# Message layers of a graph network: the next group's block numbers are read between a group's seven products

## The chip, the cores and the metric

One core of one Trainium2 chip. The metric is the device time of one execution in microseconds (us); lower is better. Three runs of the kernel before gave 5613.98, 5620.78 and 5626.88 us; their median, 5620.78 us, is the time before.

## What is computed

Four residual graph layers over 50,000 nodes with 64 features and 25,000 edges sorted by destination. The change touches the sums over edges of the first two layers (the message layers):

```python
# layer 0                                    # layer 1
messages = relu(concat(x[src], x[dst]) @ W_msg + b_msg)   ;   messages = x[src] * norm[:, None]
agg = segment_sum(messages, dst, num_segments=num_nodes)
```

The matrix products in front of layer 0's relu are made per node beforehand, so per edge only two gathered rows are added.

## The kernel before, in words

The edges lie in 200 blocks of 128, the nodes in tiles of 128. Because edges are sorted by destination, the sum over edges walks a path through (block, tile) pairs: from one item of the path to the next either the block or the tile goes up by one. There are 602 items for each layer, in 86 groups (LOTS) of seven (LOT). An item is one product: a one-hot matrix (edge lane against node lane, 128 by 128, fp32) times the block's messages (128 by 65 in layer 0, 128 by 64 in layer 1, fp32), added into one of seven slots of a PSUM bank.

`plan_items` packs each group's part of the path into one integer before the layers: the low eight bits are the group's first block number, and six more bits say for items 1 to 6 whether the block number goes up by one.

`edge_sums` is called once for each of the two layers. Its engines run side by side, tied by semaphores:

- POOL gathers the rows of four blocks at a time (a chunk; 50 chunks) with indirect DMAs, L736 and L738 in layer 0 (two per block), L741 in layer 1 (one per block). It then adds and clamps them (L748, L750) or multiplies them by a factor (L753) and raises `msg_ready` by one per chunk.
- DVE makes the seven one-hot matrices of a group in one instruction (L794, two buffers), once the products of the group before last are done, and adds the partial sum of a tile that two groups share (L800) once a group's products are done (`multiplied`).
- ACT reads the group's first tile number from a table into a register, copies that partial sum (L770), and after DVE's addition copies the group's bank into `sums` (L773), then raises `placed`.
- PE (L810 to L826) takes the group's integer from SBUF into a register (L812), clears the bank with a product of zeros (L817, which waits for `placed`), waits for the one-hots and for the chunk of the group's last block (L818 to L820), and issues seven products (L825). Both the messages' address and the slot's address of each product are computed from registers. An fp32 product runs as two passes, so seven products are 14 matmul records.

`item_blocks` (L670 to L676) builds the seven block numbers as expressions of the group's integer: mask, then for each item shift, mask and add. Register arithmetic is emitted when a value is first used. For the block numbers that is the wait at L819, whose value is the chunk of the last block. Arithmetic of neighbouring instructions is packed into one (FUSED_REGOPS in the trace) where it can be; the rest stands alone (ALU_OP). Before each product the addresses are computed at L825. All of these, with TENSOR_LOAD, SEQ_ASSERT (the check of the loaded value's bounds) and EVENT_SEMAPHORE, are instructions of PE's sequencer, which the trace marks PEldq. PE's sequencer takes its instructions in the order of the program.

The later part of the kernel (`diffuse`) uses registers that are changed in place, as the changed code does: `Counts.read` (L2077) copies such a register with `snap` before a use, and `finished` (L2080, L2081) adds one to it.

After each `edge_sums` all engines meet and `node_update` reads `sums`.

Of the kernel before, what the change touches and what calls it, by code (L numbers as in the profile page):

```python
# [29 lines left out]
CHUNKS = 2 * -(-EDGES // (2 * CH))  # L30
# [6 lines left out]
BLOCKS = EP // P  # L37
HALF = BLOCKS // 2
LOT = 7
LOTS = 2 * -(-(TILES + BLOCKS - 1) // (2 * LOT))  # L40
ITEMS = LOT * (LOTS + 1)
BLOCK_BITS = 8
# [625 lines left out]
                step(None, at(0, LAST))  # L668


def item_blocks(engine, path):

    blocks = [engine.snap((path & ((1 << BLOCK_BITS) - 1)).with_bounds(max_val=BLOCKS - 1))]
    for q in range(1, LOT):
        blocks.append(engine.snap((blocks[-1] + ((path >> BLOCK_BITS + q - 1) & 1)).with_bounds(max_val=BLOCKS - 1)))
    return blocks  # L676


def edge_sums(nc, net, layer, sums):


# [9 lines left out]
    n = f"e{layer}_"  # L691
    with ExitStack() as ctx:
        ctx.callback(nc.all_engine_barrier)
        def sb(name, shape, dt=F32):
            return ctx.enter_context(nc.sbuf_tensor(n + name, shape, dt))
# [6 lines left out]
        plan = sb("plan", [1, LOTS + 1], I32)  # L702
# [12 lines left out]
        loaded, cleared, added, msg_ready, hot_ready, multiplied, before_ready, joined, placed, pe_turn, act_turn = map(sem, names)  # L715
        n_loads = 6 if two else 5
        with nc.Block() as block:
            @block.sync
            def _(sp):
                sp.dma_start(src[:, :], net.src_cols[:, :]).then_inc(loaded, 16)  # L720
                if two:
                    sp.dma_start(dst[:, :], net.dst_cols[:, :]).then_inc(loaded, 16)
                sp.dma_start(lane[:, :], net.item_lane[:, :]).then_inc(loaded, 16)
                sp.dma_start(numbers[:, :], net.dram["c_iota"][:, 0:P]).then_inc(loaded, 16)
                sp.dma_start(plan[:, :], net.lot_plan[:, :]).then_inc(loaded, 16)
                sp.dma_start(first[:, :], net.lot_first[:, :]).then_inc(loaded, 16)
# [79 lines left out]
            @block.tensor  # L806
            def _(pe):
                pe.wait_ge(loaded, 16 * n_loads)
                pe.wait_ge(cleared, 1)
                for g in range(LOTS):  # L810
                    s = g % 2
                    path = pe.value_load(plan[0:1, g:g + 1], min_val=0, max_val=(1 << BLOCK_BITS + LOT - 1) - 1)  # L812
                    blocks = item_blocks(pe, path)
                    slots = [pe.snap((blocks[0] + q - b).with_bounds(min_val=0, max_val=LOT - 1)) for q, b in enumerate(blocks)]
                    chunk = pe.snap((blocks[-1] >> 2) + 1)
                    pe.wait_ge(placed, g + 1)
                    nc.tensor.matmul(ps[s][:, 0:LOT * wide], net.ones3[:, :], nothing[:, 0:LOT * wide], start=True, stop=False)  # L817
                    pe.wait_ge(hot_ready, g + 1)  # L818
                    pe.wait_ge(msg_ready, chunk)  # L819
                    pe.sem_inc(pe_turn, 1)  # L820
                    by_slot = ps[s][:, 0:LOT * wide].rearrange("p (u c) -> p u c", c=wide)
                    for q, (b, u) in enumerate(zip(blocks, slots)):
                        rows = msg[:, bass.ds(b, 1), 0:wide].rearrange("p b c -> p (b c)")
                        to = by_slot[:, bass.ds(u, 1), :].rearrange("p u c -> p (u c)")
                        last = nc.tensor.matmul(to, hot[s][:, q, :], rows, start=False, stop=q == LOT - 1)  # L825
                    last.then_inc(multiplied, 1)  # L826


# [1715 lines left out]
```

## Time and profile before

| what | value |
|---|---|
| median of three runs | 5620.78 us |
| the profiled execution's own time | 5624.62 us |
| its span in the profile | 5622.8 us |
| layer 0, first to last product | 836.9 to 1516.2 us |
| layer 1, first to last product | 1903.7 to 2306.0 us |
| PE / DVE / ACT / POOL busy share of the span | 60% / 48% / 19% / 50% |
| matmuls in the two stages | 2408 of 12060 |
| granted clock of PE in both stages | 0.50 |

The table's stages come from the timeline; the clock is the share of full speed that was granted, and 0.50 is the 1.2 GHz level. A line such as "L825" is a line of the kernel; "idle before <- X" says what ended the idle time of the engine in front of an instruction; "issue" means that nothing the profile shows was waited for. Records marked with a q after the engine's name are the sequencer's, and are not counted as busy.

### The profile page before, as it was taken

How to read it: one execution, taken by the hardware profiler on the slowest of the kernel's cores; microseconds unless marked ns; L12 is line 12 of the kernel's file. 1: busy time of each engine (PE TensorE's matmuls, PEld its weight loads, DVE VectorE, ACT ScalarE, POOL GpSimd, SP SyncE). 2: the span in 40 equal slices, each digit the busy share in tenths (PEclk: the TensorE clock that was granted, in tenths of full speed). 3: DMA queues.
4: the chain of work that ended last, by engine and by line, in shares of the span. 5: the costliest groups of instructions: out<-in, count | busy, mean ns of one | idle time of the engine just before them, and what ended most of it. 6: DMA issues, size and time to landing. Idle time of an engine off the chain costs nothing. (4 is left out here: it accounts for less than half of the span.)

```text
span 5622.8 us, 58211 instructions
## 1 busy us (share of the span) xinstructions
PE 3387.3 (60%) x12060; PEld 2043.7 (36%) x12060; DVE 2719.4 (48%) x6625; ACT 1086.5 (19%) x2025; POOL 2834.5 (50%) x2360
## 2 busy tenths in 40 slices
PE   3664544444499577675667665777744555555534
PEld 1222433433477466552222223555531222222212
DVE  6996551111155422364555453777774444444423
ACT  0232320101122111121222222333321111111100
POOL 0462017777511584234777772122126888787740
PEclk7776555555555555555555555555556777676765
DMA  5222430010155210252111112121112222233210
GB/s 192 82 69 100 179 118 19 19 20 20 39 151 157 52 22 13 99 210 72 23 23 23 23 23 79 70 98 79 72 61 33 30 29 30 28 31 29 28 17 3
DMA packets 350982, 346.67 MB, mean 62 GB/s; under 512 B 264934, under 2 KB 290267, under 8 KB 350835
## 3 DMA queue, kind: packets, MB, share of 16 engines
q1 hardware_dynamic: 229596, 272.37, 14.8%
q0 software_dynamic: 107888, 60.13, 8.7%
q10 hardware_dynamic: 13350, 12.40, 0.6%
q8 instruction: 69, 1.13, 0.1%
q14 instruction: 79, 0.64, 0.0%
HBM read 172.86 MB, written 175.50 MB: 62 GB/s over the span
## 5 line engine op out<-in xcount | busy, mean ns | idle before, releaser
L825 PE MATMUL e_ps<-e_msg,e_hot 128*128 x2408 | 553.9, 421 | 449.4 <-POOL e_msg L750 324.9
L825 PEld LDWEIGHTS e_ps<-e_msg,e_hot 128*128 128x128 f32 x2408 | 526.5, 330 | 522.9 <-issue 522.9
L2208 POOL DMA_INDIRECT out<-d_out,d_end x356 | 592.6, 1665 | 172.0 <-issue 167.1
L2252 PE MATMUL d_pl<-d_hot,d_fields 128*65 128x512 f32 x712 | 501.8, 870 | 0.0
L800 DVE TENSOR_TENSOR e_ps<-e_ps,e_before 128x65 f32<-128x65 f32 (+1 forms) x172 | 40.0, 233 | 871.0 <-PE e_ps L825 871.0
L736 POOL DMA_INDIRECT e_msg<-from_src,e_src x200 | 208.0, 1040 | 374.3 <-DMA e_first<-lot_first 320.3
L1971 POOL DMA_INDIRECT list<-s_rec,s_place x200 | 197.7, 988 | 290.6 <-DVE s_place L1887 234.7
L1671 POOL TENSOR_TENSOR u_tg<-u_t,norms 128x1792 f32<-128x1792 f32 x14 | 55.5, 3964 | 441.6 <-DVE u_t L1506 441.6
L1309 PE MATMUL u_po<-bias_parts,ones 3*128 3x256 bf16 x392 | 148.8, 380 | 213.7 <-issue 95.9
L741 POOL DMA_INDIRECT e_msg<-h1d,e_src x200 | 223.5, 1118 | 101.8 <-issue 54.9
L915 POOL DMA_INDIRECT a_ends<-h,a_src x200 | 220.7, 1104 | 102.7 <-issue 60.6
L738 POOL DMA_INDIRECT e_near<-from_dst,e_dst x200 | 227.1, 1136 | 61.0 <-issue 61.0
L773 ACT ACTIVATE sums<-e_ps 128x455 f32 (+1 forms) x172 | 94.0, 547 | 828.1 <-DVE e_ps L800 828.1
L1393 ACT ACTIVATE u_zt<-u_pt 128x256 f32<-128x256 f32 (+1 forms) x392 | 162.8, 431 | 461.7 <-PE u_pt L1303 461.4
L2233 PE MATMUL d_pc<-d_liveb,d_before 128*128 128x4 bf16 x89 | 14.8, 166 | 389.5 <-DVE d_prod L2350 389.1
L2252 PEld LDWEIGHTS d_pl<-d_hot,d_fields 128*65 128x65 f32 x712 | 140.1, 212 | 291.7 <-issue 291.7
L922 POOL DMA_INDIRECT agg<-a_out,a_end x200 | 204.6, 1023 | 80.5 <-issue 61.5
L2200 POOL DMA_INDIRECT d_near<-term,d_rec x196 | 190.3, 971 | 83.6 <-issue 41.8
L2244 PE MATMUL d_pr<-ident,d_scan 65*128 65x65 f32 x356 | 63.8, 334 | 275.8 <-DVE d_scan L2373 275.8
L915 POOL DMA_INDIRECT a_ends<-h,a_dst x200 | 191.5, 957 | 60.9 <-issue 60.9
L2200 POOL DMA_INDIRECT d_near<-terms,d_rec_idx x168 | 163.7, 975 | 97.5 <-DMA d_rec_w<-list_w 48.7
L2347 DVE SCALAR_TENSOR_TENSOR d_live<-d_near,d_inside 128x4 f32<-128x4 f32 x89 | 14.7, 165 | 393.4 <-DMA d_near<-term,d_rec 226.7
(359 smaller groups left out, 8152.6 us busy)
## 6 DMA issues: line engine op xcount, KB each, us to landing
u_z<-h SPq DMA_DIRECT2D x28, 896.0 KB, 6.2
x<-sums SPq DMA_DIRECT2D x28, 896.0 KB, 7.8
u_x<-x SPq DMA_DIRECT2D x28, 896.0 KB, 7.4
terms<-s_zeros SPq DMA_DIRECT2D x16, 812.5 KB, 11.8
s_key_row<-src_key SPq DMA_DIRECT2D x50, 256.0 KB
h1d<-u_h SPq DMA_DIRECT2D x14, 910.0 KB, 9.4
u_z<-h1d SPq DMA_DIRECT2D x14, 910.0 KB, 4.6
term<-u_h SPq DMA_DIRECT2D x14, 910.0 KB, 3.6
```

The lines of the kernel that those rows point to most:

```text
L736: pool.indirect_dma_start(msg[:, b, 0:C], None, net.from_src[:, :], bass.IndirectOffsetOnAxis(ap=src[:, b:b + 1], axis=0)).then_inc(gather ...
L738: pool.indirect_dma_start(near[c % 2][:, j, :], None, net.from_dst[:, :], bass.IndirectOffsetOnAxis(ap=dst[:, b:b + 1], axis=0)).then_inc( ...
L741: pool.indirect_dma_start(msg[:, b, :], None, net.h1d[:, :], bass.IndirectOffsetOnAxis(ap=src[:, b:b + 1], axis=0)).then_inc(gathered[c % ...
L825: last = nc.tensor.matmul(to, hot[s][:, q, :], rows, start=False, stop=q == LOT - 1)
L915: pool.indirect_dma_start(ends[s][:, j, half * C:(half + 1) * C], None, net.h2[:, :], bass.IndirectOffsetOnAxis(ap=rows, axis=0)).then_inc ...
L922: pool.indirect_dma_start(net.agg2[:, :], bass.IndirectOffsetOnAxis(ap=end[s][:, j:j + 1], axis=0), out[s][:, j, :], None, bounds_check=NP ...
L1309: nc.tensor.matmul(po[b][:, 0:J * C], net.ones3[:, :], net.bias_parts[:, which, :, :].rearrange("k j c -> k (j c)"), start=True, stop=False)
L1393: nc.scalar.activation(zt[b][:, :], pt[b][:, 0:TURNS * P], ACT.Copy).then_inc(zt_ready, 1)
L1971: pool.indirect_dma_start(net.lists0[:, :], bass.IndirectOffsetOnAxis(ap=place[:, t:t + 1], axis=0), rec[:, t, :], None).then_inc(scattere ...
L2200: pool.indirect_dma_start(near[s][:, j, :], None, table[:, :], bass.IndirectOffsetOnAxis(ap=row, axis=0)).then_inc(gathered[s], 16)
L2208: pool.indirect_dma_start(net.out[:, :], bass.IndirectOffsetOnAxis(ap=end[s][:, j:j + 1], axis=0), out[s][:, j, 0:C], None, bounds_check=N ...
L2252: last = nc.tensor.matmul(pl[0:WEIGHT + 1, :], fields[:, j, :], hot[:, j, :], start=j == 0, stop=j == J - 1)
```

## The change

Registers for the path, for the chunk and for two sets of seven block numbers are allocated. A new function `read_item(g, q)` takes item q of group g from the path into the set g % 2. It is called seven times before the loop for group 0, and in the loop once behind each product, for the same item of the next group. The slots' addresses are computed in place, and `item_blocks` goes.

```diff
-def item_blocks(engine, path):
-
-    blocks = [engine.snap((path & ((1 << BLOCK_BITS) - 1)).with_bounds(max_val=BLOCKS - 1))]
-    for q in range(1, LOT):
-        blocks.append(engine.snap((blocks[-1] + ((path >> BLOCK_BITS + q - 1) & 1)).with_bounds(max_val=BLOCKS - 1)))
-    return blocks
...
+                path_at = pe.alloc_register(n + "path")
+                chunk_at = pe.alloc_register(n + "chunk")
+                block_at = [[pe.alloc_register(f"{n}block{s}_{q}") for q in range(LOT)] for s in range(2)]
+
+                def read_item(g, q):
+                    row = block_at[g % 2]
+                    if q == 0:
+                        path = pe.value_load(plan[0:1, g:g + 1], min_val=0, max_val=(1 << BLOCK_BITS + LOT - 1) - 1)
+                        pe.reg_mov(path_at, path >> BLOCK_BITS)
+                        pe.reg_mov(row[0], path & ((1 << BLOCK_BITS) - 1))
+                    else:
+                        path = pe.snap(path_at, min_val=0, max_val=(1 << LOT - 1) - 1)
+                        pe.reg_add(row[q], row[q - 1], path & 1 if q == 1 else (path >> q - 1) & 1)
+                    if q == LOT - 1:
+                        pe.reg_mov(chunk_at, (pe.snap(row[q], min_val=0, max_val=BLOCKS - 1) >> 2) + 1)
+                for q in range(LOT):
+                    read_item(0, q)
                 for g in range(LOTS):
                     s = g % 2
-                    path = pe.value_load(plan[0:1, g:g + 1], min_val=0, max_val=(1 << BLOCK_BITS + LOT - 1) - 1)
-                    blocks = item_blocks(pe, path)
-                    slots = [pe.snap((blocks[0] + q - b).with_bounds(min_val=0, max_val=LOT - 1)) for q, b in enumerate(blocks)]
-                    chunk = pe.snap((blocks[-1] >> 2) + 1)
+                    blocks = [pe.snap(r, min_val=0, max_val=BLOCKS - 1) for r in block_at[s]]
                     pe.wait_ge(placed, g + 1)
                     nc.tensor.matmul(ps[s][:, 0:LOT * wide], net.ones3[:, :], nothing[:, 0:LOT * wide], start=True, stop=False)
                     pe.wait_ge(hot_ready, g + 1)
-                    pe.wait_ge(msg_ready, chunk)
+                    pe.wait_ge(msg_ready, pe.snap(chunk_at, min_val=1, max_val=CHUNKS))
                     pe.sem_inc(pe_turn, 1)
                     by_slot = ps[s][:, 0:LOT * wide].rearrange("p (u c) -> p u c", c=wide)
-                    for q, (b, u) in enumerate(zip(blocks, slots)):
+                    for q, b in enumerate(blocks):
+                        u = (blocks[0] + q - b).with_bounds(min_val=0, max_val=LOT - 1)
                         rows = msg[:, bass.ds(b, 1), 0:wide].rearrange("p b c -> p (b c)")
                         to = by_slot[:, bass.ds(u, 1), :].rearrange("p u c -> p (u c)")
                         last = nc.tensor.matmul(to, hot[s][:, q, :], rows, start=False, stop=q == LOT - 1)
+                        if g + 1 < LOTS:
+                            read_item(g + 1, q)
                     last.then_inc(multiplied, 1)
```

## Rows read from the trace of the kernel before

**Rows 1.** The page, costliest groups: busy, mean ns | idle before <- releaser.

```profile
L825 PE MATMUL e_ps<-e_msg,e_hot 128*128 x2408 | 553.9, 421 | 449.4 <-POOL e_msg L750 324.9
```

**Rows 2.** Line 825 by its source line, layer 1 alone (1900 to 2310 us).

```profile
L825 PEldq FUSED_REGOPS  x1118: 42/143/178, 1903.4 to 2304.7; - x187
its engine sat idle before it (us, times) until:
  issue: 196.0, 158
  POOL e_msg L753: 13.7, 14
```

**Rows 3.** Timeline of PE in layer 1: start us, length us, what, idle before.

```profile
1908.44 3.22 PE L825 MATMUL e_ps<-e_msg,e_hot 128*128 x14 [1.05 <-issue]
1911.60 0.55 PE L817 MATMUL e_ps<-e_nothing,ones 3*128 3x448 bf16 x1
1913.05 3.22 PE L825 MATMUL e_ps<-e_msg,e_hot 128*128 x14 [0.91 <-issue]
```

**Rows 4.** Timeline of POOL at the end of its work in layer 1.

```profile
2189.33 1.08 POOL L753 TENSOR_TENSOR e_msg<-e_msg 128x256 f32<-128x256 f32 x1 [2.56 <-DMA e_msg<-h1d,e_src]
```

**Rows 5.** One group of layer 1, PE's sequencer, 2298.15 to 2302.75 us, line by line: count, ns min/median/max, first and last start.

```profile
L825 PEldq FUSED_REGOPS  x12: 42/92/156, 2298.2 to 2300.0; - x12
...
L812 PEldq TENSOR_LOAD <-e_plan x1: 298/298/298, 2300.1 to 2300.1; - x1
...
L819 PEldq ALU_OP  x8: 32/32/36, 2300.8 to 2302.1; - x8
L819 PEldq FUSED_REGOPS  x6: 52/54/67, 2301.1 to 2302.2; - x6
...
L820 PEldq EVENT_SEMAPHORE  x1: 51/51/51, 2302.3 to 2302.3; - x1
...
L825 PEldq FUSED_REGOPS  x1: 166/166/166, 2302.5 to 2302.5; - x1
L825 PEldq ALU_OP  x1: 36/36/36, 2302.7 to 2302.7; - x1
```

**Rows 6.** Timeline around that group: start us, length us, engine, what.

```profile
2301.29 0.55 PE L817 MATMUL e_ps<-e_nothing,ones 3*128 3x448 bf16 x1
2301.47 0.23 DVE L800 TENSOR_TENSOR e_ps<-e_ps,e_before 128x64 f32<-128x64 f32 x1 [3.42 <-PE e_ps L825]
...
2301.82 0.54 ACT L773 ACTIVATE sums<-e_ps 128x448 f32 x1 [3.13 <-DVE e_ps L800]
2302.78 3.22 PE L825 MATMUL e_ps<-e_msg,e_hot 128*128 x14 [0.94 <-issue]
```

**Rows 7.** Register work elsewhere in the kernel, by source line: ns min/median/max.

```profile
L2077 PEldq FUSED_REGOPS  x89: 35/35/46, 4232.9 to 5487.1; - x89
...
L2080 DVEq FUSED_REGOPS  x89: 59/71/214, 4249.9 to 5504.0; - x89
...
L2088 PEldq FUSED_REGOPS  x10: 152/158/172, 4232.0 to 5516.4; - x10
...
L2088 DVEq FUSED_REGOPS  x10: 207/226/234, 4232.1 to 5516.3; - x10
...
L2133 PEldq FUSED_REGOPS  x10: 73/78/88, 4231.0 to 5504.0; - x10
```

**Rows 8.** Timeline of PE in the middle of layer 0.

```profile
1400.62 3.22 PE L825 MATMUL e_ps<-e_msg,e_hot 128*128 x14 [6.14 <-POOL e_msg L750]
...
1414.24 3.22 PE L825 MATMUL e_ps<-e_msg,e_hot 128*128 x14 [9.91 <-POOL e_msg L750]
```

**Rows 9.** Timeline at the end of layer 0.

```profile
1498.83 3.22 PE L825 MATMUL e_ps<-e_msg,e_hot 128*128 x14 [7.45 <-POOL e_msg L750]
...
1499.15 0.84 POOL L750 TENSOR_SCALAR e_msg<-e_msg 128x256 f32<-128x256 f32 x1 [0.19 <-issue]
...
1512.97 3.23 PE L825 MATMUL e_ps<-e_msg,e_hot 128*128 x14 [0.91 <-issue]
```

## The prediction

> **What bounds the kernel now.** The page comes first: the change touches only the two message layers, and there only PE's products of L825 and the register work around them [rows 1]. Of PE's 449 us of idle time in front of them, 325 end on a message of L750, that is, on POOL in layer 0. So layer 0 goes at POOL's pace, and PE's register work is free there except behind the last message. Layer 1 is different: by the view of that line in layer 1 alone, 196 us of idle time end on "issue" in 158 pieces, and only 13.7 us on POOL in 14 pieces [rows 2], each about 1 us, the size of the gap in every group. POOL is done at 2190.4 us [rows 4] and PE goes on to 2306.0 [rows 6]. Layer 1 is PE's own.
>
> What is it in PE? In the timeline one group starts 4.61 us behind the one before: 3.22 us of 14 passes, about 0.5 of the product of zeros, which overlaps them a little, and a gap of 0.91 us on "issue" (1.05 one group earlier, 0.94 in the last group) [rows 3, 6]. The sequencer's records of one group [rows 5] tell what the gap is. Behind the last product's issue L812 runs from 2300.1 to 2300.8, L819's 14 records from 2300.8 to 2302.3, the semaphore instruction to 2302.5, the first addresses to 2302.8, where the first pass starts [rows 6]. The other 12 address packs, two per product, take the 1.9 us from 2298.2 to the next L812. Together 4.6 us, the whole pitch: **the sequencer is never idle, and the array waits for it**. The array needs only some 3.7 us per group. Over the layer the pitch is (2302.78 - 1908.44) / 84 = 4.69 us, counting 84 groups between those two starts [rows 3, 6].
>
> From this follows how the change is to be priced. Work that is moved from one place of a serial queue to another, when the queue is what bounds, gains nothing. Only the sum of the sequencer's work per group counts, and so I count instructions.
>
> **What stays.** The load, its check and its assertion (0.7 us), the semaphore instruction, the addresses of seven products and the issues are all still there. The slot's expression is the one that was already computed at L825, so its 13 packs and one single stay. No DMA, no wait and no other engine's instruction is added or moved.
>
> **What goes.** The 14 records of L819: 1.5 us per group [rows 5]. Their executions add up to 8 x 33 + 6 x 54 = 588 ns, so each has 65 ns around it that no record shows. That is the price rule that I use: duration plus 65 ns. The counts also tell how the work is packed. Six items need 6 shifts, 6 masks and 6 additions; with the first mask and the chunk's shift and addition these are 21 operations. In 8 singles and 6 packs they fit only if each of the 7 masks stands alone, with one shift alone, and additions join shifts: a mask is never packed.
>
> **What comes**, per group:
> - Masks: 7 as before, now parted by products, alone: 7 x 0.10 = 0.70 us.
> - Item 0: a shift and a copy into the path register. The nearest row is an addition followed by a copy, 78 ns (L2133 in [rows 7]): 0.14 us.
> - Item 1: a copy of the path register by snap, alone: 0.10 us.
> - Items 2 to 6: copy and shift, a pack. Nearest: copy and addition 35 ns (L2077 in [rows 7]), addition and shift 54 ns [rows 5]: 45 + 65, 0.11 us, five times 0.55.
> - The copy of block 0 and the additions of items 1 to 5 join the address pack of the following product, which grows by one member. An address is block x width x 4 + base, the slot's number (block 0 + q - block) x width x 4 + base: eight operations in packs of six and two. These take 143 and 42 ns [rows 2], so 25 ns a member: 6 x 0.02 = 0.12 us.
> - At the group's border 12 operations meet: item 6's addition, copy, shift, addition and copy for the chunk, then seven snap copies of the block registers, which a register changed in place needs and the old expressions did not. They need two packs. The longest pack of DVE's L2080 (three additions, three copies and a product, by the program) takes 214 ns; DVE's L2088 takes 226 where PE's takes 158 [rows 7], so about 150 on PE, somewhat more for a fuller pack: 190, and 120 for the rest. With 65 each, 0.44 us.
> - The chunk's snap before the wait, alone, as it follows the wait for the one-hots: 0.10 us.
>
> Sum 2.15 us against 1.5: **+0.65 us of sequencer work per group**. The pitch becomes about 5.35 us.
>
> Bounds. Cheap end: no copy costs anything (all values used straight from their registers), and what is left are 7 masks (0.70), 6 shifts alone (0.60), additions in packs (0.14) and a pack of three for the chunk (0.13): 1.57, +0.1. Dear end: nothing joins the address packs, so 6 members cost a single each (0.60 in place of 0.12): +1.1. I take the middle case, since the rows of L2077 show such copies as instructions, and the packs as joining.
>
> **Layer 1**: 85 groups read the next one, and group 0 is read ahead of the loop, behind the wait for the cleared sums, as its integer is now; nothing covers that. All of it is the sequencer's time: 86 x 0.65 = 56 us.
>
> **Layer 0**: in the middle POOL covers it. Two groups that wait for messages start 13.6 us apart [rows 8]; a chunk of 4 blocks feeds 86 x 4 / 200 = 1.7 groups, 9 us of PE even at the new pitch. Behind the last message (end of L750 at 1500.0) four groups are worked off, with starts from 1498.83 to 1512.97 [rows 9]; three pitches grow: 3 x 0.65 = 2 us.
>
> What waits for the spread-out products? After product 0 the sequencer has about 1.3 us of load and arithmetic, after each other some 0.55 us, so a group's products end about 4.4 us after their start, not 3.2. DVE's addition and ACT's copy are over 0.9 us after that end [rows 6]; DVE's one-hots come between, and all of them serve the group after next: 5 us of room, no new wait.
>
> By these terms the profiled execution goes from its own 5624.6 us (span 5622.8) by 58 to 5683 us. The median of the runs is 3.8 us under that execution: **5679 us**.
>
> The Trainium skill, Advanced Engine Details and Errata, section Sequencer Loop, adds that other engine instructions can be read and queued while the sequencer's microcode executes one. By that rule alone moved register work would hide and the time be that of the first rival below. The rows show products queued so (the product of zeros is released by the array and not by the sequencer), but none whose own addresses are still to be computed.
>
> **Rivals.**
> 1. **The gap closes: faster.** If the sequencer were held back while seven products are in flight (by a queue in front of the array), work put there would fill lost time, and the 0.94 us gap [rows 3, 6] would go: 85 x 0.94 = 80 us, 5541. POOL would allow it: done at 2190 us [rows 4], PE then at about 2226. It decides if the sequencer has more than 0.65 us of held time among the products. For it: the gap is real, and "issue" sounds like latency. Against it: the 12 packs among the products are half of 42 and half of 143 ns, with 65 each 1.9 us in all, and the rows give 1.9 from 2298.2 to 2300.1 [rows 5]: nothing is held. The array takes 3.22 / 7 = 0.46 us per product and the sequencer 0.31, so it already runs ahead. Chance 0.07.
> 2. **It hardly matters, or it doesn't do what it says:** the compiler computes the values where they are used as before, or all copies vanish. 89 groups' worth at 0 to 0.1 us: 5621 to 5630. Against it: registers changed in place can't be read later. Chance 0.09.
> 3. **Dearer:** nothing is packed over the border of an item; 89 x 1.1 = 98, 5719. For it: a pack whose copies come late in it is slow (78 against 35 ns, L2133 against L2077 [rows 7]). Chance 0.14.
> The forecast has 0.70.
>
> **How the numbers follow.** A measurement of this kernel can tell 0.2%, 11 us, from no change. Slower by more: the forecast, rival 3 and a little: 0.84. Within 11 us: 0.08. Faster: rival 1 in full or in part, 0.08. The range reaches from the cheap end (5630) to the dear end (5719) and leaves out rival 1 and most of rival 2.
>
> **What would show it.** Right: layer 1's pitch about 5.3 us, layer 1 some 56 us longer, 14 records fewer before the wait, one or two records more behind each product, and the passes in pairs with gaps, the largest behind product 0 where the load stands; behind the product of zeros a gap of about 0.3 us instead of 0.94 (1.2 us of sequencer work behind the last product's issue, 0.9 of it under the array); layer 0 longer by about 2 us; everything behind unchanged. Wrong: a pitch under 4.69, or a layer 1 whose 14 passes still take 3.22 us while the gap shrinks.

## The result, and the profile after

The changed kernel takes 5641.2 us (median of 7 executions, 5637.8 to 5653.95) against 5620.78 (7 executions, 5613.98 to 5626.88): a ratio of 1.0039, 95% interval 1.0029 to 1.0049. The three times given for the kernel before are the lowest, the median and the highest of its seven. It is slower, as forecast, but by 20.4 us where 58 were forecast. Its profiled execution took 5641.14 us (span 5639.3).

A table by stage shows at once where that stands. The stages run from a layer's first product of zeros to its last product, and are read from the timelines; "one layer" means experiments 1 and 2 below.

| stage, us | before | after | layer 0 alone changed | layer 1 alone changed |
|---|---|---|---|---|
| ahead of layer 0 | 834.5 | 837.5 | 837.7 | 835.1 |
| **layer 0's sums** | 681.7 | **638.8** | 637.9 | 681.7 |
| between | 384.8 | 387.0 | 383.1 | 385.0 |
| **layer 1's sums** | 405.0 | **466.0** | 405.2 | 466.0 |
| all behind | 3316.8 | 3310.1 | 3311.4 | 3317.3 |
| span | 5622.8 | 5639.3 | 5575.3 | 5685.1 |

Layer 1 lost 61.0 us, and the forecast was 56. Layer 0, forecast to lose 2, **gained 42.9**. The page's line for the products [rows 1] shows both in one row:

```profile
L832 PE MATMUL e_ps<-e_msg,e_hot 128*128 x2408 | 720.6, 443 | 291.9 <-POOL e_msg L742 175.1 <-issue 110.7
```

The idle time that ends on POOL's message of layer 0 (L742 is L750 of before) fell from 325 to 175 us. Idle time that ends on "issue" did not fall: it is 110.7 us, as before. What grew is the busy column, from 553.9 to 720.6 us, since the short gaps between one product's passes and the next product's are counted there. A view by line is therefore read together with the timeline, here of PE in layer 1:

```profile
2305.57 3.49 PE L832 MATMUL e_ps<-e_msg,e_hot 128*128 x12 [0.66 <-issue]
2309.06 0.55 PE L823 MATMUL e_ps<-e_nothing,ones 3*128 3x448 bf16 x1
2309.64 0.66 PE L832 MATMUL e_ps<-e_msg,e_hot 128*128 x2
2310.92 3.68 PE L832 MATMUL e_ps<-e_msg,e_hot 128*128 x12 [0.62 <-issue]
2314.57 0.55 PE L823 MATMUL e_ps<-e_nothing,ones 3*128 3x448 bf16 x1
```

Before, 14 passes stood together in 3.22 us behind a gap of about 0.9 [rows 3, 6]. Now product 0 stands alone (0.66 us), 0.62 us of idle time follow, and the other six take 3.68 us, 0.61 each instead of 0.46. The gap behind the product of zeros is gone. The pitch (from one group's first product to the next group's) is (2326.01 - 1863.86) / 85 = 5.44 us, counted over the 85 pitches of the layer; counted in the same way before, from 1903.69 to 2302.78 us, it was 4.70: **+0.74 us per group**, 63.1 us in 85 pitches. The stage grew by 2.1 us less, since it starts with the first product of zeros, and group 0's numbers are now computed ahead of that: from there to the first product it takes 0.6 us instead of 2.7. The sequencer's records from 2309.6 to 2315.2 us, against [rows 5]:

```profile
L809 PEldq TENSOR_LOAD <-e_plan x1: 297/297/297, 2309.7 to 2309.7; - x1
...
L810 PEldq FUSED_REGOPS  x1: 98/98/98, 2310.3 to 2310.3; - x1
L811 PEldq ALU_OP  x1: 36/36/36, 2310.5 to 2310.5; - x1
L811 PEldq FUSED_REGOPS  x1: 200/200/200, 2310.6 to 2310.6; - x1
L813 PEldq FUSED_REGOPS  x5: 63/63/64, 2311.6 to 2313.9; - x5
L813 PEldq MOVE  x1: 29/29/29, 2311.1 to 2311.1; - x1
L814 PEldq ALU_OP  x6: 32/32/32, 2311.2 to 2314.1; - x6
L814 PEldq FUSED_REGOPS  x6: 169/169/213, 2311.3 to 2314.2; - x6
L821 PEldq FUSED_REGOPS  x1: 90/90/90, 2314.4 to 2314.4; - x1
L825 PEldq MOVE  x1: 29/29/29, 2314.6 to 2314.6; - x1
L832 PEldq FUSED_REGOPS  x6: 42/42/42, 2310.8 to 2313.8; - x6
```

These show all that was forecast of the packing: seven masks alone (the `ALU_OP` records of L811 and L814), five copies packed with shifts (L813's `FUSED_REGOPS`) and the first one alone (its `MOVE`), the chunk's copy alone (L825), and additions that joined the next product's addresses (L814's packs). From one load to the next there are 35 records of 3.04 us together instead of 32 of 2.47. Three records more at 65 ns each and 0.57 us more of durations make 0.77, against the 0.74 of the pitch.

Where did layer 0's gain come from? That layer goes at POOL's pace, so POOL is the engine to read. First the kernel before, POOL's costliest lines from 834 to 1502 us (busy, mean ns | idle before):

```profile
L738 POOL DMA_INDIRECT e_near<-from_dst,e_dst x192 | 219.6, 1144 | 58.6 <-issue 58.6
L736 POOL DMA_INDIRECT e_msg<-from_src,e_src x191 | 199.4, 1044 | 51.7 <-issue 51.7
L750 POOL TENSOR_SCALAR e_msg<-e_msg 128x256 f32<-128x256 f32 x49 | 41.4, 844 | 61.4 <-issue 61.4
L748 POOL TENSOR_TENSOR e_msg<-e_msg,e_near 128x256 f32<-128x256 f32 x49 | 33.9, 691 | 1.0
```

The same of the changed kernel:

```profile
L728 POOL DMA_INDIRECT e_msg<-from_src,e_src x192 | 187.3, 975 | 51.9 <-issue 51.9
L730 POOL DMA_INDIRECT e_near<-from_dst,e_dst x192 | 184.7, 962 | 58.6 <-issue 58.6
L742 POOL TENSOR_SCALAR e_msg<-e_msg 128x256 f32<-128x256 f32 x49 | 43.2, 881 | 63.6 <-issue 63.6
L740 POOL TENSOR_TENSOR e_msg<-e_msg,e_near 128x256 f32<-128x256 f32 x49 | 34.7, 708 | 1.0
```

The gathers (indirect DMAs, whose duration on POOL is that of their issue) fell from 419.0 to 372.0 us. The two arithmetic lines and the idle time in front of one of them gave back 1.8 + 0.8 + 2.2 us. The sum is -42.2 us, and layer 0's gain 42.9. And the change has no instruction on POOL. The timeline of the kernel before shows beside what the gathers took longer:

```profile
1400.28 1.03 POOL L736 DMA_INDIRECT e_msg<-from_src,e_src  x1 [0.17 <-issue]
...
1402.87 0.95 POOL L736 DMA_INDIRECT e_msg<-from_src,e_src  x1 [0.30 <-issue]
...
1404.09 1.08 DVE L794 TENSOR_TENSOR e_hot<-e_lane,e_numbers 128x896 f32<-128x896 f32 x1
1404.12 1.86 POOL L738 DMA_INDIRECT e_near<-from_dst,e_dst  x1 [0.30 <-issue]
```

Gathers of 0.95 us start every 1.25 us. One of them starts 0.03 us behind the start of DVE's one-hots and takes 1.86 us. In layer 0 of before, 60 gathers take over 1.3 us; what they take above 0.95 comes to 51 us. In the changed kernel there is none. Its timeline at the same point of a chunk:

```profile
1376.44 0.84 POOL L742 TENSOR_SCALAR e_msg<-e_msg 128x256 f32<-128x256 f32 x1 [1.20 <-issue]
...
1377.88 0.66 PE L832 MATMUL e_ps<-e_msg,e_hot 128*128 x2 [7.48 <-POOL e_msg L742]
...
1379.17 3.53 PE L832 MATMUL e_ps<-e_msg,e_hot 128*128 x12 [0.63 <-issue]
...
1382.56 0.95 POOL L728 DMA_INDIRECT e_msg<-from_src,e_src  x1 [0.30 <-issue]
...
1382.96 1.08 DVE L786 TENSOR_TENSOR e_hot<-e_lane,e_numbers 128x896 f32<-128x896 f32 x1
...
1383.81 1.05 POOL L730 DMA_INDIRECT e_near<-from_dst,e_dst  x1 [0.30 <-issue]
```

The one-hots wait for the group's products, the products wait for the message, and the message comes from POOL. So the one-hots keep a fixed distance to POOL's next gathers. The spread-out products now end 4.82 us behind their start instead of 3.22, and the one-hots start 5.68 us behind the message's end (1377.28) instead of 3.98 (1404.09 - 1400.11): 1.7 us later. At that point a gather has already been running for 0.40 us and is not held, and the next starts 0.85 us behind the one-hots and is held by only 0.1. The distance is nearly the same in every chunk: over the 47 messages that PE waits for it is 3.98 us each time in the kernel before, and 5.55 to 5.75 us, 5.61 at the median, in the changed one.

In layer 0 of the kernel before and of the changed one, a gather that starts x us behind the one-hots' start (x from 0.04 to 0.95) ends 0.81 to 0.83 us behind their end, whatever x is: it is held by about 0.95 - x. One that started ahead of them is not held. In the kernel before the border is sharp and lies where its gathers start: all those between 0 and 33 ns take 0.95 us, all from 35 ns on are held (1.87 us at 35 ns), and of the three at 34 ns one is free and two are held. Of the 60 held gathers 33 (30.1 us) belong to the first one-hots behind a message and 27 (20.8 us) to the second.

The clamping in L742 is held too, which is 1.8 us of what layer 0 gave back. In the changed kernel 18 of its 49 runs in layer 0 start 0.16 to 0.41 us before a second group's one-hots end, end about 0.70 us behind them and take up to 1.11 us instead of 0.84. Before, no run starts beside the one-hots, and all take 0.84 or 0.85. One of the 18:

```profile
1103.37 1.08 DVE L786 TENSOR_TENSOR e_hot<-e_lane,e_numbers 128x896 f32<-128x896 f32 x1
...
1104.06 1.09 POOL L742 TENSOR_SCALAR e_msg<-e_msg 128x256 f32<-128x256 f32 x1 [1.21 <-issue]
```

From here two theories compete. **A**: the hold as just told is layer 0's gain, and layer 1's loss is the sequencer's work; the two parts are independent. **B**: something else of the new order (PE's spread passes, the earlier load, a different start of the stage) speeds POOL up, and the one-hots' place goes along by chance. Four experiments (5, 6, 7 and 8) shared a chip on which the kernel before took longer too (5811.75 us). There PE's sequencer stands still for over 0.4 us at a time in layer 1 (102 times, 70 us together, in experiment 6; never in the profile of before), and code of layer 1 that is the same as before took 427, 510 and 437 us in experiments 5, 6 and 7. So layer 0 alone is read in their traces, together with its held gathers, and 7 and 8 were run again elsewhere. Ratios leave out executions in the chip's slower state, and the profiled execution of experiment 6 (5886.16 us) was one of those.

### The profile page after: what moved, and what is told of

Its sections match the earlier page's. It is cut to its first block and busy times, and to the rows that moved or that the text cites. A ratio compares the mean times of both kernels' runs of the same rounds, so it can differ in the third digit from the quotient of the medians.

```text
span 5639.3 us, 58727 instructions
## 1 busy us (share of the span) xinstructions
PE 3555.8 (63%) x12060; PEld 2115.2 (38%) x12060; DVE 2715.8 (48%) x6625; ACT 1088.9 (19%) x2025; POOL 2772.1 (49%) x2360
## 5 line engine op out<-in xcount | busy, mean ns | idle before, releaser
L832 PE MATMUL e_ps<-e_msg,e_hot 128*128 x2408 | 720.6, 443 | 291.9 <-POOL e_msg L742 175.1
L832 PEld LDWEIGHTS e_ps<-e_msg,e_hot 128*128 128x128 f32 x2408 | 602.2, 311 | 456.4 <-issue 402.0
L728 POOL DMA_INDIRECT e_msg<-from_src,e_src x200 | 194.9, 974 | 374.6 <-DMA e_first<-lot_first 320.6
L733 POOL DMA_INDIRECT e_msg<-h1d,e_src x200 | 203.6, 1018 | 101.9 <-issue 54.9
L730 POOL DMA_INDIRECT e_near<-from_dst,e_dst x200 | 192.2, 961 | 61.0 <-issue 61.0
L1670 POOL TENSOR_TENSOR u_a<-sums,u_z 128x1792 f32<-128x1792 f32 x14 | 45.4, 3243 | 337.3 <-DMA u_x<-x 337.3
```

The costliest lines, as they stand in the source:

```text
L728: pool.indirect_dma_start(msg[:, b, 0:C], None, net.from_src[:, :], bass.IndirectOffsetOnAxis(ap=src[:, b:b + 1], axis=0)).then_inc(gather ...
L730: pool.indirect_dma_start(near[c % 2][:, j, :], None, net.from_dst[:, :], bass.IndirectOffsetOnAxis(ap=dst[:, b:b + 1], axis=0)).then_inc( ...
L733: pool.indirect_dma_start(msg[:, b, :], None, net.h1d[:, :], bass.IndirectOffsetOnAxis(ap=src[:, b:b + 1], axis=0)).then_inc(gathered[c % ...
```

## The experiments

**1 and 2: each half of the change alone.** `edge_sums` takes the changed PE block for one layer and the old one for the other.

```diff
             @block.tensor
+            if two:          # experiment 2: if not two
+                ...          # PE as in the changed kernel
+            else:
                 ...          # PE as before
```

> The changed PE code in layer 0 alone, the old one in layer 1. Theory (POOL's gathers in layer 0 are held up by DVE's one-hots when a gather starts just behind the one-hots' start, and the change moved the one-hots by some 1.7 us against the gathers): layer 0 takes about 639 us instead of 682, no gather over 1.3 us, and the whole about 5578 us, faster than both kernels. Rival (the 43 us of layer 0 were chance of one execution, or belong to something else in the program): layer 0 stays at 682 and the whole at 5621 to 5623.

> The changed PE code in layer 1 alone, the old one in layer 0. Theory (PE's sequencer bounds layer 1 and has 0.74 us more to do per group): layer 1 takes 466 us instead of 405, layer 0 682 as before, the whole about 5682 us. Rival (layer 1's loss depends on when layer 0 ended or on the two together): anything else.

Measured: 5578.88 us with layer 0 changed (ratio 0.993, 0.9914 to 0.9947, to 5622.21 for the kernel before), and 5683.3 with layer 1 changed (1.0108, 1.0092 to 1.0125). The stage table has their stages: each half moves its own layer and nothing else. -43.3 and +61.1 make +17.8, against +20.4 for the whole change. So the two effects are independent, and the second run is what the forecast described: it forecast 5679 for both layers, and 5683 is what layer 1 alone does.

**3: the kernel before, with the one-hots about 0.4 us later in layer 0.** DVE waits for its own work to end (`drain`) and clears 200 columns of an unused PSUM bank in front of the one-hots. Nothing of PE is changed.

```diff
                     if not start:
                         v.wait_ge(multiplied, g)
+                        if two:
+                            v.drain()
+                            for i, w in enumerate((200,)):
+                                nc.vector.memset(idle[:, i, 0:w], 0.0)
                     nc.vector.tensor_tensor(hot[s], ...)
```

> PE's code as before; in layer 0 DVE drains and clears 200 columns of an idle PSUM bank before each one-hots, so that they start about 0.3 us later. Theory of the phase: most gathers that started 0 to 0.1 us behind the one-hots' start now start 0.2 to 0.3 us ahead of it and are not held; layer 0 gets 40 to 50 us shorter, the whole about 5575 us. Rival (the gain of layer 0 comes from PE's spread products, not from the one-hots' place): layer 0 stays within 3 us of 682.

Measured: 5614.69 us (0.9986, 0.9976 to 0.9995). Layer 0 took 662.2 us, 19.5 less: under half of the 40 to 50 that A expected, and well outside the 3 us of no change. Two stretches of its timeline say why only half:

```profile
1402.44 0.95 POOL L739 DMA_INDIRECT e_near<-from_dst,e_dst  x1 [0.30 <-issue]
1402.80 1.07 DVE L799 TENSOR_TENSOR e_hot<-e_lane,e_numbers 128x896 f32<-128x896 f32 x1
1403.70 0.99 POOL L737 DMA_INDIRECT e_msg<-from_src,e_src  x1 [0.30 <-issue]
...
1407.43 1.07 DVE L799 TENSOR_TENSOR e_hot<-e_lane,e_numbers 128x896 f32<-128x896 f32 x1
1407.50 1.82 POOL L739 DMA_INDIRECT e_near<-from_dst,e_dst  x1 [0.30 <-issue]
```

The first group behind a message is freed: the gather at 1402.44 was under way, the next starts 0.90 us behind the one-hots. But a second group often follows at once, and its one-hots, 4.63 us later, now start 0.07 us ahead of a gather. My expectation had looked at the first group alone: its held gathers fell from 33 to 1, but the second's rose from 27 to 32. Layer 0 keeps 34 long gathers (over 1.3 us) with an excess (what they take above 0.95 us) of 30 us instead of 51, and its 19.5 us of gain are those 21. The whole gained 7.5 us and not 19.5: `diffuse` took 1408.1 us in this execution and 1398.1 before, and why isn't known.

**4: the check of the loaded value's bounds is left out on PE**, in both layers, in the kernel before. It measures the price rule by itself.

```diff
-                    path = pe.value_load(plan[0:1, g:g + 1], min_val=0, ...)
+                    path = nc.values_load(plan[0:1, g:g + 1], engines=[PE], min_val=0, ..., skip_runtime_bounds_check_because=...)
```

> The kernel before without the check of the loaded path's bounds (one pack of 167 ns and one assertion of 18 ns, with what lies around them 0.35 us per group). Theory (layer 1 is bound by the sum of PE's sequencer work): layer 1 30 us shorter (86 x 0.35), layer 0 the same within 3 us, the whole about 5591 us. Rival (the idle gap of the array is a latency that register work hides under): no change within 3 us.

Measured: 5590.74 us (0.9945, 0.9928 to 0.9961). Layer 1 went from 405.0 to 377.7 us, 27.3 less, where 30 were expected. The pack and the assertion with 65 ns around each are 0.31 us per group, 27 in 86. Work taken off PE's sequencer shortens the layer by its duration and what lies around each record: the sequencer is the bound. In a row of its timeline the gap behind zeros fell from about 0.9 to 0.7:

```profile
2003.31 3.22 PE L825 MATMUL e_ps<-e_msg,e_hot 128*128 x14 [0.71 <-issue]
```

Layer 0 lost 8.9 us too, where 3 at most were expected, with 52 long gathers and an excess of 40 us instead of 60 and 51. That is the hold again. The larger part lies in the second groups, whose PE pitch is shorter by the check: their one-hots start 8.3 us behind the message instead of 8.6, and their held gathers fell from 27 to 22, with 13.4 us instead of 20.8. In the first groups 29 are held instead of 33 (26.2 us instead of 30.1), with one-hots 10 ns earlier at a border that is sharp at 34 ns.

**5: layer 0 of the kernel before almost without one-hots.** From group 2 on, DVE writes 8 columns of one one-hot matrix instead of seven whole ones; the sums of layer 0 are then wrong, and only the time is read.

```diff
+                    if two and g > 1:
+                        nc.vector.tensor_tensor(hot[s][:, 0:1, 0:8], ..., ALU.is_equal).then_inc(hot_ready, 1)
+                        return
                     nc.vector.tensor_tensor(hot[s], ...)
```

> The kernel before, but from group 2 of layer 0 on DVE writes only 8 columns of one one-hot matrix instead of all seven matrices (the rest of the one-hots is left out in layer 0). Theory (a gather of POOL that starts while DVE writes the one-hots ends 0.82 us behind them): no gather above 1.3 us in layer 0; layer 0 is shorter by the excess of the 60 long gathers, 51 us, and by some 7 us of small overlaps: about 625 to 631 us instead of 682, the whole about 5568. Rival (long gathers have another cause, such as the DMA queues or PE's traffic): they stay, and so does 682.

Layer 0 took 630.9 us. PE's order is the old one, and POOL is faster than with the change. The gathers by source line (count, ns min/median/max), first of the kernel before, then of this one:

```profile
L738 POOL DMA_INDIRECT e_near<-from_dst,e_dst x200: 940/952/1870, 810.3 to 1493.4; - x100
```

```profile
L738 POOL DMA_INDIRECT e_near<-from_dst,e_dst x200: 943/954/973, 847.3 to 1479.8; - x100
```

The median is nearly the same (952 and 954 ns) and the maximum falls, from 1870 to 973 ns: what varies is the hold. This is its whole price in layer 0, 51 us, of which the change recovered 43. (The whole kernel took 5786.26 us against 5811.75 on that chip, 0.9934, 0.9887 to 0.9981.)

**6: as experiment 3, but about 1.0 us later** (two clears of 400 columns).

> PE's code as before; in layer 0 DVE drains and clears twice 400 columns of an idle PSUM bank before each one-hots: they start about 1.0 us later. Gathers start every 1.25 us, so the next one starts about 0.2 us behind the one-hots' start and is held for 0.96 - 0.2 us. Theory of the phase: layer 0 is back at 665 to 680 us, longer than with the delay of 0.4 us (662). Rival (later one-hots are better, whatever the phase): under 660.

Layer 0 took 694.9 us, 15 to 30 more than A expected and far above the 660 of its rival: 83 long gathers, with an excess of 65 us, 14 more than before, where the layer took 13 us longer. So now both groups of a chunk are hit, 47 of the first and 35 of the second. In the timeline the message ends at 1405.04 us (1404.20 + 0.84) and the one-hots start 5.02 us later, 1.04 more than before; a gather that starts x = 0.26 us behind them takes 1.63, that is 0.95 + 0.68:

```profile
1404.20 0.84 POOL L751 TENSOR_SCALAR e_msg<-e_msg 128x256 f32<-128x256 f32 x1 [1.18 <-issue]
...
1410.06 1.07 DVE L799 TENSOR_TENSOR e_hot<-e_lane,e_numbers 128x896 f32<-128x896 f32 x1
1410.32 1.63 POOL L737 DMA_INDIRECT e_msg<-from_src,e_src  x1 [0.30 <-issue]
```

"Later" isn't better by itself; the place against the gathers' starts is what counts. The whole took 5805.01 us, 0.999 (0.9951 to 1.0029).

**7: the changed PE in layer 0, the old one in layer 1, and the one-hots another 0.8 us later** (experiment 1 with a drain and two clears of 300 columns). It tells A from B: the new order of PE stays, and only the one-hots' place goes.

> The changed PE code in layer 0, the old one in layer 1, and in layer 0 the one-hots about 0.8 us later. With the changed code gathers start 0.8 to 1.0 us behind the one-hots' start and the one before them 0.45 us ahead; now the starts fall together again. Theory of the phase: some 47 long gathers of 1.8 us, layer 0 back from 638 to about 680 us, the whole about 5620. Rival (the changed code's spread products are themselves what helps layer 0): layer 0 stays at 638 within 5 us.

Layer 0 took 675.4 us with 47 long gathers (excess 40 us), against 637.9 and none in experiment 1. The whole: 5789.34 us, 0.9956 (0.992 to 0.9991). As that chip was disturbed, the same kernel was run again elsewhere:

> The changed PE code in layer 0 with the one-hots 0.8 us later, again, where the other stages are undisturbed. Theory of the phase: layer 0 at 675 to 685 us against 638 without the delay, the whole about 5617 us. Rival (spread products help by themselves): 638, and 5579.

5614.22 us (0.9989, 0.998 to 0.9999, to 5621.02), layer 0 676.6 us, 47 long gathers, 40 us. In its timeline, 6.41 us behind the message's end:

```profile
1385.70 1.07 DVE L799 TENSOR_TENSOR e_hot<-e_lane,e_numbers 128x896 f32<-128x896 f32 x1
1385.81 1.77 POOL L739 DMA_INDIRECT e_near<-from_dst,e_dst  x1 [0.30 <-issue]
```

With PE's new order in place and only the one-hots moved onto a gather's start again, 39 of the 44 us are gone. B falls: the gain belongs to the place of the one-hots. All runs bear it out at once. Layer 0 less the excess of its held gathers is 630 to 633 us in the six kernels with PE's old order there (630.9 before, 631.5, 632.5, 632.7, 630.9 and 630.0 in experiments 2 to 6) and 635 to 639 with the new one (638.8 after, 637.9 in experiment 1, 635.4 and 636.6 here). The new order by itself is a loss of 5 to 8 us in layer 0.

**8: the parts put together.** Layer 0 takes the changed PE, for the place that it gives to the one-hots. Layer 1 keeps the old order, without the bounds check and with block numbers built without masks, so that they can be packed.

```diff
-    blocks = [engine.snap(path & 255)]                                     # every mask stands alone
+    ahead = [engine.snap(path >> BLOCK_BITS + q) for q in range(LOT - 1)] + [0]
+    blocks = [engine.snap(path - (1 << BLOCK_BITS) * ahead[0])]            # bounds left out here
     for q in range(1, LOT):
-        blocks.append(engine.snap(blocks[-1] + ((path >> BLOCK_BITS + q - 1) & 1)))
+        blocks.append(engine.snap(blocks[-1] + (ahead[q - 1] - 2 * ahead[q])))
...
+                        chunk = pe.snap(((blocks[-1] >> 2) & 63) + 1)
```

> The changed PE code in layer 0; in layer 1 the old order without the check of the path's bounds, and with the block numbers computed by shifts, products, sums and differences alone (each bit as shift minus twice the next shift), which the compiler packs, so that L819's 14 records become 6. Theory (layer 1's time is the sum of PE's sequencer records): 0.35 us less per group from the check and about 0.3 us from the packing; layer 1 about 351 to 356 us instead of 405, layer 0 at 638, the whole about 5525 us. Rival (layer 1 meets POOL's or the array's pace first, or the packs of seven are too slow): layer 1 at 375 or more, the whole at 5548 or more.

5715.78 us against 5811.75 on the disturbed chip, 0.986 (0.978 to 0.9941), with layer 1 at 366.5 us. Layer 0 took 650.9 us, not 638: 21 gathers were held, for 13 us. There PE's idle time on "issue" ahead of layer 0's products is 108.5 us instead of the 55.2 of the run below, and the first one-hots behind a message's end start 0.62 us behind it at the median (0.01 to 5.68), not 5.60. In these rows a gather starts 0.53 us behind the one-hots:

```profile
1005.77 1.08 DVE L795 TENSOR_TENSOR e_hot<-e_lane,e_numbers 128x896 f32<-128x896 f32 x1
...
1006.30 1.37 POOL L737 DMA_INDIRECT e_msg<-from_src,e_src  x1 [0.30 <-issue]
```

So the place of the one-hots, and the gain with it, depends on the chip too. Run again elsewhere:

> The combination again (changed PE code in layer 0; in layer 1 the old order, no bounds check, packable arithmetic), since in its first run the other stages too took longer than before (the attention layer 911 us instead of 799), the kernel before with them. Theory: where the attention layer takes 799 us, layer 0 takes 638, layer 1 351 to 356, and the whole is about 5525 us, 0.983 of the kernel before. Rival (PE meets POOL in layer 1): layer 1 at 366 again, the whole about 5540.

**5544.02 us** (5542.5 to 5545.31) against 5621.02, 0.9861 (0.9845 to 0.9877): faster than both kernels, by 77 and 97 us, but above the 5525 that I expected. Layer 0 took 638.0 us. Layer 1 took 362.7, where I expected 351 to 356:

```profile
2001.93 3.22 PE L866 MATMUL e_ps<-e_msg,e_hot 128*128 x14 [0.47 <-issue]
2005.08 0.55 PE L858 MATMUL e_ps<-e_nothing,ones 3*128 3x448 bf16 x1
2006.24 3.22 PE L866 MATMUL e_ps<-e_msg,e_hot 128*128 x14 [0.61 <-issue]
```

```profile
L860 PEldq FUSED_REGOPS  x340: 150/241/253, 1861.8 to 2215.2; - x170
L860 PEldq ALU_OP  x170: 36/36/36, 1862.9 to 2215.5; - x170
```

The pitch is 4.20 us over the layer. Each of the 85 groups in this window has four packs and two singles on this line, the 6 records that I expected, where L819 had 14 [rows 5], but three of the packs take 230 to 253 ns. Against experiment 4, packing gave 377.7 - 362.7 = 15 us, a little over half of the 26 (86 x 0.3) that I counted on: eight records went, at 65 ns each 0.52 us, but their durations rose from 588 ns to 955.

## Why the prediction was right, and where it was wrong

**Right: what bounds layer 1.** "The sequencer is never idle, and the array waits for it": work moved from ahead of the products to between them brought nothing, and the layer grew by the sum of what was added. Experiment 4 shows the same in the other direction: 0.31 us less per group, and 27.3 us less for the layer. Rival 1, the gap that closes for a gain, fell: the 0.94 us gap did close, to 0.03 us where 0.3 was forecast, and came back as 0.62 us behind product 0 and 0.15 us more at each of the others. The Trainium skill (Advanced Engine Details and Errata, Sequencer Loop) says that other engine instructions can be read and queued while the sequencer's microcode executes. That did not hide these records here, with +0.74 us per group: each product's own addresses stand behind them.

**Right: the price of the sequencer's work.** +0.65 us per group was forecast, +0.74 measured, and +56 us for the layer against +61.0. The count was exact, 17 records for 14, and the packs were those forecast. What was short is the durations: item 0's pack 98 ns (78 taken), the pack behind it 200 (168), copy and shift 63 (45), five times. Item 6's pack took 213 ns for 190 and the next 90 for 120.

**Right, small: layer 0's tail.** From POOL's end of messages to the last product it took 16.2 us before (1500.00 to 1516.19) and 18.4 after (1457.85 to 1476.26): +2.2, with 2 forecast.

**The step that failed** is the one for layer 0: "in the middle POOL covers it". It took POOL's pace as given. POOL's pace depended on PE through DVE: 60 held gathers in 86 groups. The change pushed the one-hots by 1.7 us relative to the gathers, and with them went 47 us of POOL's gather time. The +2 of the tail stood, and -45 was missing. The paragraph on the waiting engines had the very fact ("a group's products end about 4.4 us after their start, not 3.2"; it is 5.0 in layer 1 and 4.8 in layer 0) and asked only whether anybody would be late. Nobody was. What it didn't ask is what else an instruction of DVE meets when it starts at another time. The clue stood in the trace of before: two kinds of duration on one line, gathers of the same form with a mean of 1144 ns on L738 and 1044 on L736, of which most take 952.

None of the rivals named this, and all of them let layer 0 stand. The sum with both layers' measured terms is -42.9 + 61.0 = +18; the other stages differ by +3.0, +2.2 and -6.7 us, -1.5 together, and the medians by 20.4. That 5641 us still lies between the 5630 and 5719 of the forecast is luck: that range was built from prices of the sequencer's work, none of its terms moves layer 0 by more than some 3 us. With the one-hots at the place of experiment 7 the same sum is 676.6 - 681.7 + 61.0 = +56 us.

## What to carry to other kernels

When a change stretches or shifts work on one engine, ask not only who waits for it but which instructions of other engines start relative to it, and what they then overlap: an engine that "covers" may owe its pace to that. Look for one line with two durations in the trace (minimum, median, maximum) and for what runs beside the long ones; here moving 86 instructions of DVE by 0.8 us cost 39 us (experiment 7), over half of what all the register arithmetic of the change cost. A gain that hangs on such a place is fragile: the same kernel had no held gather in layer 0 on one chip and 21 on another. And where the sequencer is the bound, count records and their durations, not positions: only taking work away helps.

## What the runs showed of the hardware

- **POOL's instructions are held by DVE's one-hots.** The one-hots compare two SBUF tables for 1.08 us. In layer 0 of the kernel before, gathers of 0.95 us that start 0.04, 0.11, 0.35, 0.41, 0.62 and 0.89 us behind them take 1867, 1794, 1551, 1493, 1272 and 1012 ns, 1.9 - x each; all 60 that start 35 ns or more behind them end 813 to 831 ns behind the one-hots' end. Where the gather is the first behind a message and takes 1.04 us by itself, the end comes 0.90 to 0.91 us behind (experiment 8, first run). Its border at 34 ns has been told. With DVE's clears directly ahead of the one-hots (experiments 3, 6 and 7) the border lies elsewhere: in experiment 3 gathers are held that start up to 98 ns ahead of the one-hots, and those 142 ns ahead are not; in experiment 6 two that start 170 and 183 ns ahead are held and one at 182 is not. Why was not tried. The Trainium skill (SBUF — State Buffer, Who interferes with whom) says that a DVE instruction with two SBUF inputs contends with a GpSimd instruction that reads SBUF, since both use one read interface. A gather has its indices in SBUF, and POOL's clamping, which is held too, reads the messages there: these runs agree. The same section reports that `tensor_tensor` did not stall a DMA in the original probe; here it holds gathers, by 0.92 us at most in the kernel before. That the hold comes from these reads, and whether DVE's write has a part in it, was not tried by itself.
- **The effect of a delay goes up and down, and fits the gathers' pitch of 1.25 us.** Layer 0 took 682, 662, 695, 638 and 677 us with the first one-hots later by 0, 0.4, 1.0, 1.6 and 2.4 us (medians; the last two with PE's new order). The gathers of the first group are held 33, 1, 47, 0 and 47 times: freed at 0.4 and at 1.6, which are 1.2 apart, and held at 1.0 and 2.4.
- **Register work of PE's sequencer** comes to its duration and 65 to 69 ns per record (65 within L819's records, 69 over a whole group of layer 1 before): a single or a copy takes 29 to 36 ns, copy and shift 63 or 64, the longer packs 90 to 253. The seven masks of a group stood alone in the kernel before and in the changed one.
